# Edge pass of a graph transformer layer: softmax chunks of eight half groups, values in a ring of cells

## What is computed

```python
# graph attention, 4 heads of 64
q, k, v = x @ Wq + bq, x @ Wk + bk, x @ Wv + bv            # x: normed nodes + mean edge embedding
alpha = sum(q[dst] * k[src], axis=-1) / 8                  # per edge and head
a     = exp(alpha - segment_max(alpha, dst)[dst])
out   = segment_sum(a * v[src], dst) / (segment_sum(a, dst) + 1e-16) + x @ Ws + bs
# a mixing branch (linear attention, norm, two layers of 768 with gelu), added
# then norm, softmax router and 8 experts of three layers on every node, added
```

## Time and profile before

| | us |
|---|---|
| median of 3 runs | 2798.48 (2795.07 to 2813.19) |
| the profiled execution's own time | 2799.82 |
| its span, first to last instruction | 2798.1 |
| TensorE busy | 2449.6 |
| VectorE busy | 2136.1 |
| ScalarE busy | 1389.5 |
| GpSimd busy | 928.6 |
| mean granted TensorE clock | 0.954 of full speed |

### The profile page before, as it was taken

How to read it: one execution, slowest core, us unless ns; L and a number is a source line. 1 busy time by engine, 2 the same in 40 slices (tenths; PEclk the granted TensorE clock), 3 DMA queues, 4 the chain that set the end, 5 groups by cost and what they waited for, 6 DMA issues and landing times.

```text
span 2798.1 us, 42202 instructions
## 1 busy us (share of the span) xinstructions
PE 2449.6 (88%) x13352; PEld 2052.8 (73%) x13352; DVE 2136.1 (76%) x3853; ACT 1389.5 (50%) x2619; POOL 928.6 (33%) x891
## 2 busy tenths in 40 slices
PE   6478994798899889889988989867999999999998
PEld 4257773677677677767767767646988888888898
DVE  6797542898889989889898898867666666666665
ACT  5421110465565565656555656545555555555554
POOL 0140004566566666656666666600000000000000
PEclk9689997899999999999999999987999999999999
DMA  5031456566666666666666666630000000000000
GB/s 158 24 115 38 137 179 194 163 196 191 195 192 194 207 181 195 202 186 196 199 197 184 194 203 192 193 115 16 14 16 16 16 16 16 16 16 14 14 9 12
DMA packets 189688, 336.30 MB, mean 120 GB/s; under 512 B 31112, under 2 KB 128688, under 8 KB 189446
## 3 DMA queue, kind: packets, MB, share of 16 engines
q0 software_dynamic: 67104, 219.09, 26.3%
q1 hardware_dynamic: 122374, 114.53, 13.6%
HBM read 293.84 MB, written 40.48 MB: 119 GB/s over the span
## 4 chain that ended last, share of the span: by engine, by line
PE 66%; DVE 21%; issue 7%; another core or an unknown queue 3%; DVEq 1%; ACT 1%; DMA 0%; POOL 0%; SPq 0%; ACTq 0%; POOLq 0%
PE ps L1389 19%; PE ps L1399 10%; PE ps L1285 10%; PE ps L1274 7%; PE ps L1150 5%; DVE ring L1737 4%; PE ps L1245 3%; PE ps L1252 3%; DVE ring L1789 2%; DVE rows L1486 2%; PE ps L1230 2%; PE ps L1063 1%; DVE nodes L1803 1%; PE ps L1070 1%
## 5 line engine op out<-in xcount | busy, mean ns | idle before, releaser
L810 POOL DMA_INDIRECT ring<-kv_rows,idx x832 | 875.4, 1052 | 757.3 <-issue 267.2
L1274 PE MATMUL ps<-nodes,ohT 128*128 x1664 | 423.0, 399 | 101.7 <-issue 56.9
L1389 PE MATMUL ps<-f_split,e_up 128*128 128x512 f32 (+1 forms) x1664 | 503.6, 384 | 6.7 <-DVE e_low L1950 6.3
L1274 PEld LDWEIGHTS ps<-nodes,ohT 128*128 128x128 f32 x1664 | 322.9, 199 | 176.3 <-issue 128.9
L1285 PE MATMUL ps<-ring 128*128 128x260 f32 x1664 | 437.7, 408 | 0.0
L1926 DVE TENSOR_TENSOR f_split<-f_more,f_split 128x1024 fp32r<-128x1024 f32 (+1 forms) x208 | 242.0, 1164 | 238.4 <-ACT f_split L995 234.9
L989 ACT ACTIVATE f_more<-ps,e_rest 128x512 f32<-128x512 f32 (+1 forms) x416 | 289.5, 747 | 268.7 <-PE ps L1389 267.9
L1389 PEld LDWEIGHTS ps<-f_split,e_up 128*128 128x128 f32 x1664 | 307.1, 191 | 55.0 <-DVE e_low L1950 7.0
L1285 PEld LDWEIGHTS ps<-ring 128*128 128x128 f32 x1664 | 311.5, 197 | 41.2
L922 ACT ACTIVATE nodes<-ps 128x780 f32 x208 | 170.8, 821 | 314.6 <-PE ps L1285 248.9
L1389 PE MATMUL ps<-f_split,e_low 128*128 128x512 f32 (+1 forms) x832 | 316.4, 380 | 0.0
(11 more groups left out here) (347 smaller groups left out, 3472.9 us busy)
## 6 DMA issues: line engine op xcount, KB each, us to landing
relq<-rel_rows SPq DMA_DIRECT2D x208, 128.0 KB
ring<-kv_rows,idx POOLq DMA_INDIRECT x832
kv_rows<-work SPq DMA_DIRECT2D x49, 256.0 KB, 2.2
xn_rows<-nodes SPq DMA_DIRECT2D x1, 6272.0 KB, 22.4
sx_rows<-work SPq DMA_DIRECT2D x49, 128.0 KB, 1.7
nodes<-in_x_dram SPq DMA_DIRECT2D x4, 1536.0 KB
work<-in_x_dram SPq DMA_DIRECT2D x48, 128.0 KB, 2.3
m_xn<-xn_rows SPq DMA_DIRECT2D x24, 256.0 KB
```

The lines of the kernel that those rows point to most:

```text
L810: pool.indirect_dma_start(out=kvh(c)[:, g, 0:2 * D], out_offset=None, in_=kvD, in_offset=bass.IndirectOffsetOnAxis(ap=idx[c // KP][:, s:s ...
L1274: last = pe.matmul(ps[:, 2048 + D * g:2048 + D * (g + 1)], ohT[c % 2][:, g * P:(g + 1) * P], nodes[:, ds(win[g] * AC + HG * AC, D)], start ...
L1389: last = pe.matmul(bank(2 * l + m, 0, n * P), e_parts[l][w][:, e, i, m * P:(m + 1) * P], src_[a][:, i * QW:i * QW + n * P], start=(i == 0 ...
```

## The change

**Chunks.** `CH` goes from 4 to 8, so a chunk is 32 columns, 128 rows, and there are 26 chunks. `LAG` is now `CH + 3 = 11`. The chain of runs is `4 * 33 = 132` wide in place of 68; its tables have one buffer instead of two and are loaded by `tab_load` four steps into a chunk.

**Cells.** Slots are gone. For each of the four columns `ring` has 22 cells of 260 numbers; half group `i` begins at cell `4 * i % 21`. Keys take nearly one cell and values with their weights the next, and keys live 5 half groups (until the scores), values 16. So a later half group's rows are gathered over dead keys between values that are still alive. A gather waits for the sum of half group `i - 16` and for the scores of `i - 5`. The arrival is counted on 6 semaphores.

**One-hots.** The column one-hots go to two buffers `keys` of their own. The weights are spread to the cells by `spread_weights`, one instruction for each run of rising cells.

**PSUM.** The ends of rows go to banks 1 and 3 instead of bank 0 at partition 64; the chain's copy also waits for `acc_copied`.

**Elsewhere.** The experts' weights have a semaphore each, the third set is loaded last, after the last sum, and two fills of `zeros` and `tab` are made by GpSimd at its third gather.

```diff
-    KP = 12
-    CH = 4
+    KP = 16
+    KEYS = 5
+    KVS = 6
+    CELLS = 21
+    LOT = (CELLS + 1) * AC
+    CH = 8
...
-    LAG = 7
-    AHEAD = 4
+    LAG = CH + 3
+    WL = H * (CS + 1)
...
+    def cell(i):
+
+        return 4 * i % CELLS
...
-        PS_END = bank(0, AC, AC + P)[64:65, :]
+        PS_END = [bank(b, AC, AC + CS * H)[0:1, :] for b in (1, 3)]
+        PS_ENDS = ps[0:1, 512:512 * 5].rearrange("p (a x) -> p a x", a=2)[:, :, AC:AC + CS * H]
...
+                if c % CH == 4 and (not known or i < NHF):
+                    k = m * (U // CH) + c // CH
+                    if k == 0:
+                        sp.wait_ge(sem("pass_zero"), 2)
+                    else:
+                        sp.wait_ge(sem("carry_made"), k)
+                    tab_load(k)
...
-            sp.wait_ge(sem("agg_ps"), NHF - 10)
-            weights(2, Wo)
-            sp.wait_ge(sem("agg_ps"), NHF - 4)
-            sp.wait_ge(sem("diff_made"), NCH)
-            weights(1, W2)
+            sp.wait_ge(sem("qg_ps"), NHF)
+            sp.wait_ge(sem("al_T"), NCH)
...
+            res_load(0)
+            sp.wait_ge(sem("diff_made"), NCH)
+            weights(1, W2)
+            sp.wait_ge(sem("agg_ps"), NHF)
+            weights(2, Wo)
...
-                if not isinstance(i, int) or i >= KP:
+                if i >= KP:
                     pool.wait_ge(sem("agg_ps"), i - (KP - 1))
-                elif i > AHEAD:
-                    pool.wait_ge(sem("prod_made"), i - AHEAD)
+                if i >= KEYS:
+                    pool.wait_ge(sem("alpha_made"), i - (KEYS - 1))
+                if i == 2:
+                    pool.memset(zeros[:, :], 0.0).then_inc(sem("pass_zero"), 1)
+                    pool.memset(tab[:, :], BIG_NEG).then_inc(sem("pass_zero"), 1)
...
-            def sum_keys(j, cj):
-                kv = kvh(cj)
+            def sum_keys(j):
+                key = keys[j % 2]
                 for g in range(HG):
-                    ins = act.activation(kv[:, g, 0:P], iota_f[:, :], ACT.Abs, bias=relC[:, ds(j * HG + g, 1)], scale=-1.0)
+                    ins = act.activation(key[:, g * P:(g + 1) * P], iota_f[:, :], ACT.Abs, bias=relC[:, ds(j * HG + g, 1)], scale=-1.0)
...
+            def spread_weights(k):
+                lots = ring[:, :].rearrange("p (g c a) -> p c g a", g=HG, a=AC)
+                ex = PS_EX.rearrange("p (h n g) -> p n g h", h=H, g=HG)
+                first = 0
+                for u in range(1, CH + 1):
+                    if u == CH or cell(k * CH + u) < cell(k * CH + u - 1):
+                        at = cell(k * CH + first) + 1
+                        ins = act.activation(lots[:, at:at + 4 * (u - first - 1) + 1:4, :, D - H:D], ex[:, first:u], ACT.Copy)
+                        first = u
+                ins.then_inc(sem("a_made"), 1)
...
-            def carries(k, b, go):
+            def carries(k, go):
...
+                dve.wait_ge(sem("tab_in"), 48 * (k + 1))
                 dve.wait_ge(sem("ends_T"), k + 1)
+                if k >= 1:
+                    dve.wait_ge(sem("acc_copied"), k * CH + (CH + 1) - LAG)
```

More of the change, by code:

```diff
@@ L85, in gps_layer_kernel, with row_cells @@
     ORDER_GAPS, ORDER_FLAG, SLOT_KEYS, SLOT_COLS, SLOT_ROW, X_VAR, X_SHIFT, GRAM_ZERO = range(1, 9)
+    def cell(i):
+        return 4 * i % CELLS
+    def row_cells(i):
+        return range(AC * cell(i), AC * cell(i) + D), range(AC * cell(i) + D, AC * cell(i) + SL)
+    for i in range(CELLS):
+        for d in range(1, 2 * CELLS):
+            new = range(AC * cell(i + d), AC * cell(i + d) + SL)
+            for old, life in zip(row_cells(i), (KEYS, KP)):
+                assert d >= life or new[-1] < old[0] or old[-1] < new[0]
     def done(g):
@@ L264, in gps_layer_kernel @@
         wrow, slot_w, base_w = [row_box[32 * i:32 * i + 1, 0:n].bitcast(U32) for i, n in ((1, NSP), (2, NSP), (3, NHF))]
-        tab = [row_box[0:1, 210 * b:210 * (b + 1)] for b in range(2)]
-        links_row = row_box[0:1, 420:560]
-        run_f = row_box[0:1, 560:630]
-        run_b = row_box[0:1, 630:702]
-        carry = row_box[0:1, 702:702 + 2 * CS * H]
-        open_m = row_box[0:1, 830:830 + 2 * H]
+        WE2 = WL + 2
+        tab = tab_box[0:1, :]
+        links_row = row_box[0:1, 0:2 * WE2]
+        run_f = row_box[0:1, 2 * WE2:3 * WE2]
+        run_b = row_box[0:1, 3 * WE2:4 * WE2 + 2]
+        carry = row_box[0:1, 4 * WE2 + 2:4 * WE2 + 2 + 2 * CS * H]
+        open_m = row_box[0:1, 4 * WE2 + 2 + 2 * CS * H:4 * WE2 + 2 + 2 * CS * H + 2 * H]
+        assert 4 * WE2 + 2 + 2 * CS * H + 2 * H <= NSP
         def bank(i, a=0, b=512):
@@ L927, in step @@
                 if not known or 0 <= i - LAG < NHF:
-                    sum_keys(i - LAG, (c - LAG) % U)
-                if c % CH == 3 and (not known or i >= 7 and i - 7 < NHF):
-                    kk = m * (U // CH) + (c - 7) // CH
+                    sum_keys(i - LAG)
+                if c % CH == 3 and (not known or i >= LAG and i - LAG < NHF):
+                    kk = m * (U // CH) + (c - LAG) // CH
                     act.wait_ge(sem("ex_T"), kk + 1)
@@ L1275, in spread_q, with gather_up @@
                 last.then_inc(sem("qg_ps"), 1)
-            def gather_up(j, cj, place, width):
+            def gather_up(j, place, width):
                 for g in range(1, HG):
@@ L1284, in gather_up @@
                     to = ps[:, ds(place[g - 1] * 512, AC)] if g else bank(0, 0, AC)
-                    last = pe.matmul(to, kvh(cj)[:, g, 0:P], kvh(cj)[:, g, D:SL], start=(g == 0), stop=False, skip_group_check=True)
+                    last = pe.matmul(to, keys[j % 2][:, g * P:(g + 1) * P], kvh(j)[:, g, D:SL], start=(g == 0), stop=False, skip_group_check=True)
                 last.then_inc(sem("agg_ps"), 1)
@@ L1321, in step @@
                     last.then_inc(sem("carry_T"), 1)
[L1322 to L1324 removed]
+                if c % CH == 2 and (not known or i >= CH + 2 and i - (CH + 2) < NHF):
+                    pe.wait_ge(sem("open_ex"), k(CH + 2) + 1)
+                    pe.wait_ge(sem("ex_made"), k(CH + 2) + 1)
                     pe.sem_inc(sem("begun"), 1)
@@ L1328, in step @@
                 if not known or 0 <= i - LAG < NHF:
-                    gather_up(i - LAG, (c - LAG) % U, place, AC if known and i == LAG else 4)
+                    gather_up(i - LAG, place, AC if known and i == LAG else 4)
                 if win:
                     spread_q(i + 2, c + 2, win)
-            pe.wait_ge(sem("acc_zero"), 5)
             spread_q(0, 0, windows_of(0))
@@ L1813, in step @@
                 ch = lambda d: (c - d) % U // CH
-                if c % CH == 2 and (not known or i >= 6 and i - 6 < NHF):
+                if c % CH == 2 and (not known or i >= CH + 2 and i - (CH + 2) < NHF):
                     sums_seen(i)
-                    go, _ = chained("schain", k(6) * 9 + 5)
-                    differences(k(6), ch(6) % 2, go)
+                    go, _ = chained("schain", k(CH + 2) * 9 + 5)
+                    differences(k(CH + 2), ch(CH + 2) % 2, go)
                 if not known or 0 <= i - LAG < NHF:
```

142 lines of the change are left out of this document (67 added, 75 removed).

## The result

The kernel before took 2805.1 us (median of 20 runs), the changed one 2788.5 us (20 runs): ratio 0.9946, 95% interval 0.9928 to 0.9963. That is some 17 us by the medians, 15 by the ratio. The forecast was 68 us less, 2731, with a range of 2684 to 2776. The gain is real and much too small: outside the range, and within 1% of the kernel before.

A forecast was written before the change was run, and what follows sets the result against it. VectorE and TensorE, nearly equally loaded and coupled, were taken to bound the edge pass. -94 (chunks and pace) + 14 (longer lag) + 9 + 3 (new waits) = -68 us, so 2731 us, range 2684 to 2776.

The forecast's parts named there:

- Part 1: Half as many softmax chunks in the edge pass: VectorE saves 0.48 us of work a half group, 100 us.
- stalls at L1778: VectorE's waits before the first scan of the differences, 0.89 us each: half to go, 12 us.
- Part 2: TensorE is late next in the edge pass: gain between TensorE's sum, 77 us, and VectorE's, 112; taken as 94.
- Part 3: LAG 7 to 11: more half groups with only scores or only sums at the pass's ends, 14 us more, at most 25.
- Part 4 (a): The chain's copy newly waits for ScalarE's copy of the windows: 0.35 us a chunk, 9 us; bounds nothing and 151.
- (b): Weights go to scattered cells by more ScalarE instructions, VectorE's weighing waits for the last: 3 us; bounds 0 and 12.
- (e): The third layer's weights load after the last sum: hidden; without that cover 11 us.
- (c): Gathers also wait for the scores five half groups back; lead the same both times: cost nothing.
- the first paragraph's reading: In the edge pass VectorE and TensorE, nearly equally loaded and coupled, each lose 0.7 to 0.8 us a half group to one another.
- Rival 2: TensorE sets the edge pass's pace and the waits grow: -20 us, 2779 us; chance 0.10.
- Rivals 1, 3 and 4: VectorE alone sets the pace, 2701 us, 0.16; chain waits a whole round, 2870, 0.06; wider chunks gain nothing, 2813, 0.03.

The follow-up runs named there:

- e16: The kernel before with the values' half of each gathered row left out from half group 24 on: 2727.8 us, ratio 0.9987.
- e13: The changed kernel itself, unedited, run again in the set where the kernel before takes 2731 us: 2655.7 us, ratio 0.9731.
- e6: e4 with the chain's row ends back in bank 0, no wait for ScalarE's copy, and two table buffers: 2881.9 us, ratio 1.0311.
- e8: e4 with the chain's ends and tables, and the gathers' release, as in the kernel before: 2790.6 us, ratio 1.0028.
- e17: e4 run again, in the set of 2785 us: 2935.3 us, ratio 1.0539.
- e18: e4 with the gathers released as in the kernel before, in the set of 2785 us: 2811.5 us, ratio 1.0099.
- e1: The changed kernel with SHIFT = 5 for 3, the dense branch two half groups later against the chunks: 2805.0 us, ratio 1.0004.
- e4: The changed kernel with CH = 4 and LAG = 7 again, all the rest of the change kept: 2917.6 us, ratio 1.0352.
- e12: The kernel before with the values' half of each gathered row left out from half group 24 on: 2731.0 us, ratio 0.9998.
- e10: The changed kernel with each gather released one half group later, two half groups ahead of the products: 2661.3 us, ratio 0.9752.
- e15: The changed kernel with the values' half of each gathered row left out from half group 24 on: 2654.2 us, ratio 0.9726.

## Why the prediction was right and wrong

The terms of the sum, between the starts and ends of the pass. From the first product to the last, and from the last product to the last copy of windows, whose rows are, for the first set (before, after) and for e16 and e13:

```profile
1840.73 1.21 DVE L1737 TENSOR_TENSOR ring<-ring,ps 128x1024 f32<-128x1024 f32 x1
```

```profile
1823.51 1.21 DVE L1774 TENSOR_TENSOR ring<-ring,ps 128x1024 f32<-128x1024 f32 x1
...
1880.65 0.82 ACT L960 ACTIVATE nodes<-ps 128x780 f32 x1 [2.40 <-PE ps L1321]
```

```profile
1768.15 1.20 DVE L1737 TENSOR_TENSOR ring<-ring,ps 128x1024 f32<-128x1024 f32 x1
...
1811.90 0.82 ACT L922 ACTIVATE nodes<-ps 128x780 f32 x1 [2.40 <-PE ps L1285]
```

```profile
1683.85 1.22 DVE L1774 TENSOR_TENSOR ring<-ring,ps 128x1024 f32<-128x1024 f32 x1
...
1741.05 0.82 ACT L960 ACTIVATE nodes<-ps 128x780 f32 x1 [2.40 <-PE ps L1321]
```

The last copy of the kernel before is at 1884.81; the first products start at 446.59, 442.89, 440.99 and 439.93.

| | forecast | first set | e16 to e13 |
|---|---|---|---|
| first to last product (parts 1, 2, 4) | -94 + 9 + 3 = -82 | 1394.1 to 1380.6, -13.5 | 1327.2 to 1243.9, -83.2 |
| last product to last copy (part 3) | +14 | 44.1 to 57.1, +13.1 | 43.8 to 57.2, +13.5 |
| kernel, medians | -68 | -17 | -75 (e13 against before) |

- **Part 1**, VectorE's saving of 0.48 us a half group: right. 1014.71 / 169 = 6.00 us became 991.67 / 180 = 5.51. The chain's scans took 420 and 397 ns (0.41 forecast). The copy took 412 for 285 ns, the two scans together 0.27 us more and the two adds 0.13 (281 and 274 for 215 and 206 ns), 0.53 in all, where 0.52 was taken. The slow slope of the scan, on which the prediction cited the Trainium skill ("DVE: opcode table, instruction layouts, handler registers and perf-mode slots", section 6), is in these rows again: 64 columns more for 0.13 us each.
- The stalls at L1778, of which half were to stay: all went (13.4 us in e16, 0.0 at L1818 in e13).
- **Part 2**, a pace between the two engines' sums: right without disturbance. e16 is the kernel before with the gathers' bytes halved, which moved its time by 0.1%. 1100 / 180 = 6.11 us a half group, 6.2 forecast, TensorE at 1015.64 / 180 = 5.64 us of work, 5.72 forecast. Its waits before the chunk's matmuls fell from 46.9 + 17.0 us (L1314, L1320) to 1.7 + 3.8. That VectorE would wait for TensorE instead shows at L1843: 36.0 us.
- **Part 3**: right, +13 in both pairs.
- **Part 4 (a)**: 10.6 / 23 = 0.46 us a chunk, 0.35 forecast, 12 us in place of 9; in the first set 22.1 / 21 = 1.05 us, 27 us in place of 9. **(b)** VectorE's weighing waits 0.2 us for the weights in e13's stretch. **(e)** hidden: the experts' weights are first read 24.1 us after the last copy of windows in the first set (1904.75 after 1880.65), as before. **(c)**, "cost nothing": the lead is the old one, as said. But e6 against e8 and e17 against e18 show that the release has a large price where it differs: 91 (79 by the ratios) and 124 us for one half group of lead. The forecast kept no bound for that.

**The step that failed** is the first paragraph's reading, on which part 2 stands: that the two engines lose 0.7 to 0.8 us "to one another", all of it, so that the idle time answers to the other engine's work and shrinks with it. Idle us a half group in the stretch, in the disturbed set and without disturbance:

| | before | changed | e16 | e13 |
|---|---|---|---|---|
| TensorE | 0.79 | 0.75 | 0.62 | 0.47 |
| VectorE | 0.69 | 1.07 | 0.50 | 0.60 |

Without disturbance the reading fits: TensorE's idle time falls by 0.15 us and VectorE's grows by 0.10. In the disturbed set TensorE's stays and VectorE's grows by 0.38. From the first product to the last, the kernel before takes 1394.1 - 1327.2 = 67 us more there than without disturbance, the changed one 1380.6 - 1243.9 = 137: the loss doubles, of the -82 us some 70 went to it, and the sum has no term for it. The five long stalls are some 30 of the 137 us; the rest is spread over shorter waits and TensorE's slower matmuls (975.25 / 167 = 5.84 us of work a half group, 5.64 in e13). The sign stood in the rows quoted: 16.4 of the 36.4 us at L1778 and 3.7 at L1700, 39.3 of the 241.9 at L922 and 26.8 at L810 are "remote".

In e13's set the change gives 75 us where 68 were forecast, which bears out the terms of the sum; the number on record was for a kernel of some 2800 us, and there it missed. Rival 2 named the nearest time, 2779, and its sign was there (TensorE idle (1100 - 975.25) / 167 = 0.75 us a half group, VectorE idle more), but its mechanism, TensorE's work as the floor, isn't what the runs show: the same kernel runs at 6.11 us in e13. Rivals 1, 3 and 4 fell: VectorE does wait for TensorE, no wait of a whole round stands before the chain (longest 0.7 us in e13, 2.8 in the first set), and wide chunks do cut the cost.

Open: what makes TensorE's results late. It comes with the set of runs, not the kernel alone, since the same kernel shows 0 or 273 us of it. The number of the chip doesn't settle it: chip 3 is on record both for the set of 2806 us (e1 to e4) and for that of 2731 (e13 to e16). How much it costs does depend on the kernel: by the medians of different sets the kernel before loses 2805 - 2731 = 74 us to it, the changed one 2789 - 2656 = 133. Why is only argued: VectorE was the longer engine before (5.93 against 5.84 us), with some slack for late results; now it waits for each of them. That the transfers' load or timing feeds it is likewise argued, from the gathers' release alone; the halved gathers would tell, but met no disturbed set.

## What to carry to other kernels

Before a sum is made from a profile of a program on one core, look for waits with no releaser of its own ("remote"), and for waits of TensorE on "issue". Here they marked a disturbance in that execution; their sum didn't say what it cost. Price the change once without it, once with it growing, and let the range hold both. And keep the kernel itself in each set of experiments: three edits gave 0.974 to 0.975 here, and so did no edit.

## What the runs showed of the hardware

- One kernel, several paces: 2731 to 2732, 2783 to 2785 or 2805 to 2806 us for the kernel before, by set. Its granted clock is 0.98 in the stretch in the first set and 0.98 in e12 and e16 alike, the changed kernel's 0.97 against 0.98 in e13. The difference is in results that arrive up to 7.5 us after the recorded ends of the matmuls.
- Where that happens, gathers that started four half groups ahead of their product and not three cost 79 to 124 us, with the same bytes and the same work. Where it doesn't, two ahead and not three cost at most some 5 us (e10), and halving the bytes of the gathers from half group 24 on (0.70 to 0.45 of the DMA engines' time, e13 and e15) changed the time by 0.1%.
- After the stall shown above the granted clock was 0.93 in 1260 to 1264 us and 0.64 in 1264 to 1268, so TensorE, which had no matmul for 4.4 us before it, was at its lower level (1.2 GHz) for part of the time: 2.87 us for matmuls that else take 1.89. That stall cost more than its length.
